# New call orders on all five engines of a gated linear-attention and FFN layer

## The reference

```
q, k, v = x@Wq, x@Wk, x@Wv;  fg = sigmoid(x@Wf + bf)          # 16 heads of 8 dims
state = state * fg[..., None] + v[..., None] * k[..., None, :]  # per token, per head 8x8
out   = einsum('bhij,bhj->bhi', state, q)
out   = layernorm(out) * gamma + beta
x     = layernorm(x + (out * silu(x@Wg)) @ Wout)
h     = silu(lin(x, w1)) * lin(x, w2)                            # 128 -> 512
h     = gelu(lin(h, h1));  h = gelu(lin(h, h2))                  # 512 -> 512, twice
x     = layernorm(x + lin(h, w3))                                # 512 -> 128
```

## Time and profile before

| | |
|---|---|
| median of 3 runs | 525.56 us (523.36 to 525.65) |
| profiled execution | span 520.7 us from first to last instruction, 7950 instructions |
| median less span | 4.9 us |
| granted TensorE clock | 0.999 of 2.4 GHz |
| DMA | 87.33 MB, mean 168 GB/s |

### The profile page before, as it was taken

How to read it: one execution, slowest core, us unless ns; L and a number is a source line. 1 busy time by engine, 2 the same in 40 slices (tenths; PEclk the granted TensorE clock), 3 DMA queues, 4 the chain that set the end, 5 groups by cost and what they waited for, 6 DMA issues and landing times. The chain is left out here.

```text
span 520.7 us, 7950 instructions
## 1 busy us (share of the span) xinstructions
PE 502.3 (96%) x2524; PEld 382.6 (73%) x2524; DVE 453.9 (87%) x707; ACT 403.9 (78%) x837; POOL 317.8 (61%) x363
## 2 busy tenths in 40 slices
PE   8999999999999999999999999999999998999995
PEld 5466777787876767787877777687767777767885
DVE  4699899999999998999999989999998999991462
ACT  3567778789797688889888787889788878678754
POOL 0642755839394765938295775858496775838351
PEclk9999999999999999999999999999999999999999
DMA  6987998972998748895597963699947747400001
GB/s 197 257 230 165 250 230 217 230 166 77 211 232 218 174 133 199 211 237 162 128 233 196 265 167 70 166 228 234 237 108 196 180 131 177 107 1 2 21 22 43
DMA packets 21500, 87.33 MB, mean 168 GB/s; under 512 B 2512, under 2 KB 3280, under 8 KB 13520
## 3 DMA queue, kind: packets, MB, share of 16 engines
q1 hardware_dynamic: 21312, 86.53, 66.7%
q10 hardware_dynamic: 144, 0.26, 0.1%
HBM read 74.72 MB, written 12.06 MB: 167 GB/s over the span
## 5 line engine op out<-in xcount | busy, mean ns | idle before, releaser
L474 POOL TENSOR_TENSOR h1lo<-h,h1hi 128x512 fp32r<-128x512 f32 x60 | 77.7, 1313 | 27.4 <-ACT h1hi L891 27.1
L898 ACT ACTIVATE h<-F,cols 128x512 f32<-128x512 f32 x120 | 79.0, 686 | 9.4 <-PE F L2303 8.9
L542 POOL TENSOR_TENSOR QJ<-QJ 128x512 f32<-128x512 f32 x14 | 18.0, 1285 | 102.6 <-DVE QJ L1589 102.6
L474 POOL TENSOR_TENSOR h2lo<-h,h2hi 128x512 fp32r<-128x512 f32 x60 | 76.1, 1298 | 5.6 <-ACT h2hi L891 5.5
L1574 DVE TENSOR_TENSOR_SCAN KJ<-g,KJ 128x512 f32<-128x512 f32 x64 | 74.8, 1203 | 3.7 <-POOL KJ L523 3.2
L1574 DVE TENSOR_TENSOR_SCAN KJ<-g,carry,KJ 128x512 f32<-128x512 f32 x64 | 77.8, 1261 | 0.3 <-ACT carry L824 0.2
L2303 PE MATMUL F<-h2hi,whi 128*128 128x512 f32 (+1 forms) x256 | 73.4, 421 | 1.8 <-DVE h2hi L1694 1.0
L1581 DVE TENSOR_TENSOR QJ<-QJ,KJ 128x1024 f32<-128x1024 f32 x60 | 75.0, 1275 | 0.0
L2303 PE MATMUL F<-h1hi,whi 128*128 128x512 f32 (+1 forms) x256 | 69.8, 413 | 3.8 <-DVE h L1638 3.8
L2303 PE MATMUL F<-h1lo,whi 128*128 128x512 f32 (+1 forms) x256 | 67.1, 404 | 0.0
L2303 PE MATMUL F<-h2lo,whi 128*128 128x512 f32 (+1 forms) x256 | 66.0, 400 | 0.0
(11 more groups left out here) (176 smaller groups left out, 947.7 us busy)
## 6 DMA issues: line engine op xcount, KB each, us to landing
KJ<-qk_bounce SPq DMA_DIRECT2D x30, 1024.0 KB, 11.2
QJ<-qk_bounce SPq DMA_DIRECT2D x30, 1024.0 KB, 11.4
qk_bounce<-qk SPq DMA_DIRECT2D x30, 256.0 KB, 3.1
x_in<-in_x SPq DMA_DIRECT2D x16, 256.0 KB, 7.8
xT<-in_xT SPq DMA_DIRECT2D x15, 256.0 KB, 4.6
out<-res SPq DMA_DIRECT2D x15, 256.0 KB, 3.1
wraw<-in_wffn SPq DMA_DIRECT2D x2, 1024.0 KB, 10.5
wraw<-in_wffn SPq DMA_DIRECT2D x2, 256.0 KB, 4.3
```

The lines of the kernel that those rows point to most:

```text
L474: e.tensor_tensor(h_lo[layer][:, t, :w], h[:, t, :w], h_hi[layer][:, t, :w].bitcast(f32), ALU.subtract).then_inc(lo_done[layer], 1)
L542: e.tensor_tensor(first, first, other, ALU.add).then_inc(add_gp_done, 1)
L898: e.activation(dst[:, t, :WIDTH[n]], F[t][:, :WIDTH[n]], ACT.Gelu, scale=scale[t]).then_inc(gelu_done[layer], 1)
```

## The change

All five lists are put in another order, from the first block to the last. The calls are the same, with the same arguments, as often; every function but those below is the same. The waits for a freed bank or a read tile are now looked up in two tables.

```diff
+            XT_READ = {
+                4: (qj_made, 8), 5: (gate_made, 2), 6: (q_made, 2), 7: (gate_made, 4), 8: (gate_made, 5), 9: (gate_made, 6), 10: (gate_made, 7), 11: (gate_made, 8), 12: (gate_made, 9), 13: (gate_made, 10), 14: (gate_made, 11), 15: (gate_made, 12),
+            }
             def load_xT(n):
                 if n >= XTB:
-                    done, value = {4: (qj_made, 8), 6: (q_made, 2), 9: (v_made, 6)}.get(n, (gate_made, n - 3))
-                    e.wait_ge(done, value)
+                    xT_read(n)
...
-            def freed(n, usual, others):
-                done, value = others.get(n, usual)
-                if value:
-                    e.wait_ge(done, value)
+            def freed(use, n):
+                if n in FREED[use]:
+                    e.wait_ge(*FREED[use][n])
...
-                freed(n, (gate_done, n), {1: (kvj_done, 1), 2: (tanh_done, 2), 4: (q_copied, 3), 5: (q_copied, 5), 9: (tanh_done, 9), ...
+                freed("k", n)
```

The beginning, VectorE and ScalarE (TensorE's order up to `rest` is unchanged):

```diff
             qsj(6)
+            find_low_parts()
             scan(0, 7)
             kv(1, 0)
             qsj(7)
...
             stats_1(0)
+            qs(1, 0)
             scan(1, 5)
+            half_norm("1")
             scan(1, 6)
-            find_low_parts()
             set_flag()
-            half_norm("1")
-            qs(1, 0)
+            scan(1, 7)
             x1_lo(0)
             qs(1, 1)
-            scan(1, 7)
             qs(1, 2)
             hmul(0, 0)
```

More of the change, by code:

```diff
@@ L367, in _ @@
             send(6, 0)
-            store(1)
-            load_xT(8)
[L370 to L375, removed]
+            load_x(7)
+            fetch(6, 1, 1)
+            fetch(6, 0, 0)
+            fetch(6, 0, 1)
+            store(2)
+            send(7, 1)
+            load_x(8)
+            fetch(7, 1, 0)
+            fetch(7, 1, 1)
+            load_xT(8)
+            load_xT(9)
@@ L390, in _ @@
+            fetch(9, 1, 0)
             fetch(8, 0, 1)
-            send(9, 1)
+            load_xT(12)
+            fetch(9, 1, 1)
+            load_x(10)
             send(9, 0)
-            load_xT(10)
+            send(10, 1)
             store(4)
-            load_xT(11)
             fetch(9, 0, 0)
[L397 to L403, removed]
+            send(10, 0)
@@ L668, in _ @@
             lo(2, 6, 2)
+            rstd_of(7, "1")
             lo(2, 6, 3)
-            rstd_of(7, "1")
+            kv_gp(9, 6)
+            kv_gp(9, 7)
+            rstd_2(5)
             add_gp(8)
@@ L983, in _ @@
             tanh(0)
+            sum_low_parts(0)
             g_of_tanh(0)
@@ L986, in _ @@
             copy_qj(0)
+            sum_low_parts(1)
             copy_kj(2)
@@ L1019, in _ @@
             silu(0, 0)
-            save_carry(1)
+            g_of_tanh(2)
             silu(0, 1)
+            silu(0, 2)
+            copy_v(2)
             hi(1, 0, 0)
-            g_of_tanh(2)
-            silu(0, 2)
+            silu(0, 3)
             hi(1, 0, 1)
-            silu(0, 3)
             hi(1, 0, 2)
+            center_w3()
+            copy_q(3)
             hi(1, 0, 3)
-            copy_q(3)
-            center_w3()
             norm_o(1)
@@ L1201, in _ @@
             gelu(1, 5, 3)
+            copy_v(8)
             hi(2, 5, 3)
@@ L1278, in _ @@
             silu(8, 0)
-            copy_v(10)
-            silu(8, 1)
+            copy_k(11)
             hi(1, 8, 0)
             g_of_tanh(10)
+            silu(8, 1)
+            norm_2(6)
             hi(1, 8, 1)
@@ L1949, in _ @@
             residual_2(6)
-            kv(9, 0)
+            scan(9, 0)
             hmul(7, 2)
@@ L2099, in _ @@
             scan(14, 6)
-            scan(14, 7)
-            qs(14, 0)
             qs(14, 1)
             qs(14, 2)
+            scan(14, 7)
+            add(14, 0)
+            kv(15, 0)
+            qs(14, 3)
             x1_lo(13)
-            add(14, 0)
-            qs(14, 3)
             add(14, 1)
@@ L2267, in sum_transposed @@
                 terms = HD if n in EARLY else 1
-                freed(n, (r2_done, n - 1), {1: (x1lo_done, 1)})
+                freed("sum", n)
                 for c in chunks(n):
@@ L2406, in last_begin @@
                     e.wait_ge(w3_centered, 1)
-                freed(n, (x1lo_done, n + 2), {})
+                freed("last", n)
                 for k in range(NH - 1):
```

1186 lines of the change are left out of this document (598 added, 588 removed).

## The result

The changed kernel takes 558.16 us (557.37 to 558.9, 4 runs) against 525.49 us (523.36 to 525.65, 4 runs): 1.064 times as long, 95% interval 1.060 to 1.068. I had forecast 521 us, with 529.5 as the upper end. It is slower by 32.7 us where I expected 4.5 us less.

What follows compares the result with a forecast made beforehand. TensorE, busy 96%, was taken as the bound, with VectorE (87%) second nearly full. Terms -2.8 - 1.2 - 1.0 = -5.0 us gave 515.7 + 4.9 = 520.6, said as 521 us; range 516 to 529.5, forecast's own 518.5 to 522.9.

Steps and rivals of the forecast that it cites:

- VectorE, steady stretch: 60 to 450 us: recurrence ahead of FFN work lets VectorE win waits back; -2.8 us, ends +3.6 and -10.
- Here a page bears on it ... I follow the rows: Tail: the page's rule would stretch two subtractions, 2 x 0.54 us, winning nothing; by the rows 1.0 us is won.
- VectorE late: Slower rival: x1_lo(n) and hmul(n,t) from block 1 on come late, VectorE not catching up; 530 us, chance 0.14.
- a transfer late: Slower rival: fetch(9,0,1) behind send(10,0) on SyncE, and its like, 2 us late twice; 527.5 us, 0.07 past the bound.
- the subtractions in the tail at 800 ns and more: Sign of being wrong: VectorE's subtractions beside GpSimd's in the tail last that long, against 417 to 426 ns before.
- The three waits: Steady stretch: VectorE's waits for x1hi, attention output and summed transpose, 5.0 + 4.1 + 2.8 us, fall under 4 of 11.9.
- what it can win back: Steady stretch: VectorE's 11.9 us of waits, about 0.9 us in each of 13 or so blocks, pay for the shift.
- Start, -1.2: Start of kernel: TensorE reaches the product at 53.24 about 1.2 us sooner; ends +1 and -2.5 us.
- part (c): Start: scan(1,7) ahead of x1_lo(0), first qs ahead of both; hmul(0,0) at about 51.2 instead of 52.44.
- all three: Start: low_any sums and find_low_parts earlier, half_norm("1") before scan(1,6), and scan(1,7) earlier; one chain, 1.2 us all told.
- Tail, -1.0: Last block, layer 2: TensorE's 1.03 us wait for VectorE's third cast goes; -1.0 us, part behind last product unchanged, 5.5 us.
- Tables, transfers: FREED and XT_READ tables, table loads and xT's transfer, issued blocks ahead: all costed at nothing.

Runs made afterwards that it cites:

- the two kernels with reductions: VectorE's qs and add replaced by reductions with one SBUF operand, orders untouched: 515.05 us with the orders of after, 519.75 us with those of before.
- the run with the tail alone: Kernel before, with the last calls of VectorE, ScalarE, TensorE and GpSimd in the order of the kernel after: 522.57 us against 523.84, ratio 0.999.
- the 42 calls ahead of scan(n,7): Kernel after, with reductions in place of only the 42 of 102 qs and add calls standing before scan(n,7): 524.93 us.
- the phases above: Two kernels of their own, not the block: VectorE and GpSimd instructions, eight each, alone and side by side; SBUF product and difference together took 17.7 us.
- the second regrouping: Kernel after, with qs and add put from before scan(n,7) to behind it, and behind x1_lo(n-1) where that follows within three calls: 577.93 us.
- five moved products: Kernel before, with five VectorE qs products moved out of meetings with GpSimd: 526.65 us, ratio 1.007; with the tail of the kernel after too: 526.67 us, 1.009.

## Why the prediction was wrong

*The step that failed* is "VectorE, steady stretch", -2.8 us with ends +3.6 and -10, together with its sentence "Here a page bears on it ... I follow the rows". I counted the moved operations at their duration alone and never asked what ran on GpSimd beside their new places. The term that was missing is +37.3 us (43.1 of meetings after, less 5.8 before), ten times the bad end. No rival held it either: the slower ones were VectorE late (530) and a transfer late (527.5, where its own terms, 521 + 4 + 2, give 527).

*The rows that I followed did not bear on the question.* I argued that VectorE's four h2lo subtractions of the earlier trace rows are not stretched though both operands lie in SBUF. Their places on VectorE, then GpSimd's, in the kernel before:

```profile
502.92 0.42 DVE L1699 TENSOR_TENSOR h2lo<-h,h2hi 128x256 fp32r<-128x256 f32 x1
503.25 2.31 DVE L1694 CAST h2hi<-h 128x256 fp32r<-128x256 f32 x3
505.60 0.76 DVE L1699 TENSOR_TENSOR h2lo<-h,h2hi 128x256 fp32r<-128x256 f32 x2
```

```profile
503.08 2.33 POOL L480 TENSOR_TENSOR h2lo<-h,h2hi 128x256 fp32r<-128x256 f32 x3 [3.03 <-DVE h2hi L1694]
```

Two ended at 503.34 or before, two began at 505.60 or later, and GpSimd worked from 503.08 to 505.41: only its first subtraction began inside one of VectorE's, by 0.26 us, and that one is 856 ns and its followers 782 and 774. The group's minimum and maximum could not show a meeting, because there was hardly one. The same VectorE line for layer 1 had one, in the same trace of the kernel before; below it the layer 2 line of the kernel after:

```profile
L1699 DVE TENSOR_TENSOR h1lo<-h,h1hi x4: 412/416/857, 493.7 to 497.3; 128x256 fp32r<-128x256 f32 x4
```

```profile
L1707 DVE TENSOR_TENSOR h2lo<-h,h2hi x4: 411/646/964, 537.0 to 540.7; 128x256 fp32r<-128x256 f32 x4
```

The h1lo of 857 ns began at 497.34, inside GpSimd's h1lo of 497.18 to 497.92. In the kernel after, two of the four h2lo subtractions take 865 and 964 ns beside GpSimd's: the last sign of being wrong that I had named ("the subtractions in the tail at 800 ns and more") came, and the rule held in the tail as well. Only its price there did not follow, since TensorE no longer waits at that cast. Evidence against the rule would have had to be a pair that overlaps; and the qs durations of the trace before (1.87, 1.97, 2.15 and 2.19 us, where one alone takes 1.22) held pairs for it.

The Trainium skill, GPSIMD Engine Reference, Key points, names the contention "with two SBUF inputs"; the runs agree (2244 and 2146 ns against 1262 and 1220). The Trainium skill, SBUF — State Buffer, Who interferes with whom, goes further, and the runs agree in each point that a phase tried: the pair is an exclusive lock, a GpSimd instruction that only writes is left alone (525 ns), a reduction never contends (1212 ns).

*The rest of the working, with the meetings off* (the two kernels with reductions, spans 513.4 and 517.4 us). Waits of VectorE from 60 to 450, orders of after, then of before:

```profile
DVE h L1646 <- ACT h L893: 7.7, 15, 1.0
...
DVE x1lo L1641 <- ACT x1hi L886: 1.8, 3, 0.9
...
DVE stats_o L1601 <- PE back L2293: 1.0, 2, 0.8
DVE x_in L1636 <- PE back L2311: 0.8, 2, 0.6
```

```profile
DVE x1lo L1633 <- ACT x1hi L878: 5.2, 8, 0.9
DVE x_in L1628 <- PE back L2289: 4.1, 6, 1.4
DVE stats_o L1593 <- PE back L2271: 2.9, 4, 1.1
DVE h L1638 <- ACT h L885: 2.4, 7, 0.7
```

The first waits of TensorE for `hmul` in the two, in the same order:

```profile
50.71 0.74 PE L2325 MATMUL F<-x1hi,whi 128*128 128x512 f32 x2 [0.61 <-DVE h L1646]
```

```profile
51.86 0.73 PE L2303 MATMUL F<-x1hi,whi 128*128 128x512 f32 x2 [1.21 <-DVE h L1638]
```

- Steady stretch, -2.8. The three waits go from 12.2 to 3.6 us; I had written under 4 of 11.9. TensorE's idle from 60 to 450 is 3.0 us (387.02 busy) against 4.1; I had written 2 to 3. x1_lo(15) ends at 479.4 against 483.4, 4.0 us sooner, where I had 4.0 for stretch and start together. But VectorE did not win its waits back: 5.3 of these 8.6 us came back as its wait for ScalarE's silu (2.4 to 7.7 us), and it is busy 370.8 us of the 390 against 370.2. It comes to `hmul` before its input is there; that is how TensorE's wait for `hmul` in this stretch went from 3.3 to 0.7 us. The size was right, the reason ("what it can win back") only in part.
- Start, -1.2. x1_lo(0) ends at 47.7 us in both kernels with reductions, so nothing was won up to there, but TensorE reaches the product behind the first `hmul` at 50.71 and not at 51.86, 1.15 us sooner: part (c) of my working gave what I had for all three. With the meetings on it is 52.66 against 53.24. The low_any operation that I took at 0.66 us had itself been held; in the kernel after it takes 172 ns.
- Tail, -1.0: x1_lo(15) to the end is 34.0 us in both. The wait of 1.0 us at the third cast went; up to the last product 0.4 us are left of it (27.5 against 27.9), and the part behind the last product, which I had as unchanged, is 6.5 against 6.0. Why, no run shows, and the run with the tail alone doesn't tell it from nothing.
- Tables, transfers: no wait of VectorE for a landing of Q or K in the kernel after is in the steady stretch's list; with meetings off, three of 1.8 us in all. That rival was not what happened.

That the 4.7 us between the kernels with reductions (4.0 by their spans) agree with the -5.0 of the forecast so closely is in part luck: the start and the steady stretch hold by their sizes, the tail gave nothing.

*Why 39.6 us on an engine that is 64% busy cost TensorE 26 us.* GpSimd's share of time was no measure. lo(2,n,·) is on the chain gelu, hi, lo, product, with TensorE waiting at its end, and rstd is on the way to x1. An instruction on such a chain that lasts 1 us longer can delay the product by 1 us whatever the engine does the rest of the time: 19.2 of TensorE's 30.7 us are waits for h2lo. And a late GpSimd can then meet the next qs. That lateness breeds meetings I infer from the counts (31 long ones after; 10 when the 42 calls ahead of scan(n,7) can't meet, against 7 before); no run took it apart.

## What to carry to other kernels

Before a VectorE instruction with two SBUF operands (or a cast or tensor_scalar from SBUF to SBUF, as in the phases above) is moved, look at what GpSimd does at its new place: if both read SBUF they run one after the other, and the chain that TensorE waits for can pay for it. Put such instructions where GpSimd waits, or take one operand from PSUM: kv did that, and giving it up cost 38 us with no call moved. Fewer meetings alone are not enough: in three runs here (the second regrouping, VectorE's old list in the new kernel, five moved products) there were fewer, and the time rose. And test a rule against a row only where the row holds the case that the rule speaks of.

## What the runs showed of the hardware that I had not expected

- VectorE 128x1024 product of SBUF tiles beside GpSimd 128x512 difference: 2.20 us from start to start for each pair; alone 1.14 and 1.22, which would be 2.36 one after the other.
- GpSimd's 4-column product: 199 ns beside a reduction, 1186 beside the 128x1024 product; a 4-column addition 3.58 us beside three products in a row.
- VectorE's cast fp32 to fp32r of 128x512: 421 ns alone, 1480 beside GpSimd; the tensor_scalar 540 and 1479.
- GpSimd's fill of 128x512: 525 ns, untouched; its tensor_scalar with one SBUF operand, 1577 a piece, from start to start 1.55 us beside the product of 1.14, so held too (alone it was not run).
